# Normalising an octet's attention output in four steps of 128 columns instead of one step of 512

## The reference

```python
xn = _layernorm(x)
x = x + attn0(xn, Wq, Wkv, Wo, bo) + ffn0(xn, ln_w, gate_w, up_w, down_w)
xn = _layernorm(x)
x = x + attn1(xn, Wq, bq, Wk, bk, Wv, bv, Wo, bo) + ffn1(xn, W_gate, W_up, W_down)

# in each attention, for every head
scores  = where(causal, q @ k.T, -inf)
weights = softmax(scores / sqrt(16))
ctx     = weights @ v            # the division by the softmax sum is the step of this case
```

## Time and profile before

| what | us |
|---|---|
| median of 3 runs | 890.82 (888.83 to 896.04) |
| the profiled execution, its own time | 892.07 |
| its span | 889.6 |
| TensorE busy in matmuls | 832.2 (94%) |
| VectorE busy | 607.8 (68%) |
| mean granted TensorE clock | 0.982 of full speed |

### The profile page before, as it was taken

How to read it: one execution, slowest core, us unless ns; L and a number is a source line. 1 busy time by engine, 2 the same in 40 slices (tenths; PEclk the granted TensorE clock), 3 DMA queues, 4 the chain that set the end, 5 groups by cost and what they waited for, 6 DMA issues and landing times.

```text
span 889.6 us, 16314 instructions
## 1 busy us (share of the span) xinstructions
PE 832.2 (94%) x5611; PEld 629.0 (71%) x5612; DVE 607.8 (68%) x1584; ACT 462.0 (52%) x828; POOL 416.0 (47%) x551
## 2 busy tenths in 40 slices
PE   8889999989999898999998998999898998999995
PEld 4866666768867665777787865776578775666785
DVE  7756557797765968666877688575668766665545
ACT  2433555566644555545665465445465564544662
POOL 3233444446444653454443644454355545544543
PEclk9999999999999999999999999999999998999999
DMA  6672363534526263636564274656565384733231
GB/s 204 167 165 73 98 130 129 102 133 78 158 82 165 84 145 101 128 135 128 180 105 173 73 161 139 119 174 103 180 116 162 110 154 148 137 112 102 83 103 48
DMA packets 61841, 113.08 MB, mean 127 GB/s; under 512 B 8760, under 2 KB 11832, under 8 KB 61752
## 3 DMA queue, kind: packets, MB, share of 16 engines
q1 hardware_dynamic: 61760, 112.05, 49.1%
HBM read 87.30 MB, written 24.64 MB: 126 GB/s over the span
## 4 chain that ended last, share of the span: by engine, by line
PE 76%; DVE 15%; issue 3%; ACT 2%; POOL 2%; DMA 1%; POOLq 0%; SPq 0%; ACTq 0%; DVEq 0%
PE g_ring L1226 37%; PE acc L1226 21%; PE s_bank L1339 7%; PE g_ring L1379 6%; PE t_bank L1359 4%; DVE o_t L1215 4%; DVE s_bank L1196 3%; DVE h_lo L1175 2%; DVE x L1183 1%; DVE qk_parts L1134 1%; POOL x L955 1%; DVE context L1216 1%; DVE xn L1111 1%; PE g_ring L1263 1%; POOL w_lo L945 1%
## 5 line engine op out<-in xcount | busy, mean ns | idle before, releaser
L945 POOL TENSOR_TENSOR w_lo<-w_raw,w_hi 128x512 fp32r<-128x512 f32 x204 | 271.3, 1333 | 155.2 <-ACT w_hi L987 150.6
L1196 DVE CUSTOM_DVE_ANT_0 s_bank<-s_bank,causal 128x128 f32<-128x128 f32 (+3 forms) x512 | 236.9, 519 | 36.4 <-PE s_bank L1339 35.9
L967 POOL TENSOR_SCALAR_AFFINE_SELECT p<-p 128x256 f32<-128x256 f32 (+1 forms) x320 | 121.9, 382 | 295.3 <-ACT p L980 288.3
L1226 PE MATMUL g_ring<-xt_hi,w_hi 128*128 128x512 f32 (+1 forms) x504 | 210.8, 418 | 6.2 <-DVE xt_lo L1125 3.2
L1226 PE MATMUL g_ring<-xt_lo,w_hi 128*128 128x512 f32 (+1 forms) x504 | 199.2, 395 | 0.0
L1226 PE MATMUL g_ring<-xt_hi,w_lo 128*128 128x512 f32 (+1 forms) x504 | 198.4, 394 | 0.0
L980 ACT ACTIVATE p<-t_bank 128x512 f32<-128x512 f32 x320 | 173.8, 595 | 36.5 <-PE t_bank L1359 29.7
L987 ACT ACTIVATE w_hi<-w_raw 128x512 fp32r<-128x512 f32 x204 | 127.2, 628 | 112.9 <-PE g_ring L1226 77.7
L1226 PE MATMUL acc<-w_hi,h_hi 128*128 128x256 f32 (+1 forms) x528 | 157.0, 297 | 9.0 <-DVE x L1183 4.9
L1226 PE MATMUL acc<-w_lo,h_hi 128*128 128x256 f32 (+1 forms) x528 | 150.4, 285 | 0.0
L1226 PE MATMUL acc<-w_hi,h_lo 128*128 128x256 f32 (+1 forms) x528 | 150.3, 285 | 0.0
(11 more groups left out here) (86 smaller groups left out, 845.3 us busy)
## 6 DMA issues: line engine op xcount, KB each, us to landing
w_raw<-weights_in SPq DMA_DIRECT2D x204, 256.0 KB, 3.1
qk_scratch<-qk_parts SPq DMA_DIRECT2D x24, 512.0 KB, 2.9
q_op<-qk_scratch SPq DMA_DIRECT2D x96, 128.0 KB, 4.6
o_scratch<-o_t SPq DMA_DIRECT2D x32, 256.0 KB, 3.1
k_op<-qk_scratch SPq DMA_DIRECT2D x48, 128.0 KB, 7.0
context<-o_scratch SPq DMA_DIRECT2D x16, 256.0 KB
o_t<-o_scratch SPq DMA_DIRECT2D x16, 256.0 KB
k_op<-k_scratch SPq DMA_DIRECT2D x48, 64.0 KB, 5.4
```

The source lines that it names most:

```text
L945: pool.tensor_tensor(w_lo[:, c % SPLIT, :], w_raw[:, c % RAW, :], w_hi[:, c % SPLIT, :].bitcast(F32), ALU.subtract).then_inc(split_done, 1)
L967: pool.affine_select(out=view, in_=view, compare_op=ALU.is_ge, fill=0.0, base=0, pattern=[[0, n], [1, P]] if n == 2 else [[1, P]], channel ...
L1196: last = dve.tensor_tensor_reduce(out=bank[:, at:at + n], in0=bank[:, at:at + n], in1=causal[:, 512 - n:], scale=1.0, scalar=LOWEST, op0=A ...
L1226: ins = pe.matmul(dst, w[a], xa[c], start=first and i == 0, stop=last and i == 2, skip_group_check=skip)
```

## The change

The step "norm" of an octet becomes four steps, one for each 128 columns. Each part waits for the same arrival of the read as before, takes its own reciprocal, waits for it, multiplies its own 128 columns, and counts `norm_done` up. The users of a normalised tile wait for the fourth part. In the planner each part is a step of its own, with a cost of 1.35 us where the whole step had 1.3; the four are placed one after the other, each from the planned end of the one before. The expected time of the write to `o_scratch` goes from 5.0 to 4.0 us and that of the read from 10.0 to 8.0. All other steps and their shapes are as they were, but the planner writes all five lists anew.

```diff
-          "norm": 1.3, "hlo": 0.7}
+          "norm": 1.35, "hlo": 0.7}
...
-O_WRITE, O_READ = 5.0, 10.0
+O_WRITE, O_READ = 4.0, 8.0
...
+NORM_PARTS = 4
...
             here = place("sp", free, "oin", octet) + O_READ
-            end["norm", octet] = place("dve", here, "norm", octet)
+            for part in range(NORM_PARTS):
+                end["norm", octet] = here = place("dve", here, "norm", octet, part)
...
-    n_norm = by(numbered(VE, "norm"), 1)
+    n_norm = {s[1]: n for s, n in numbered(VE, "norm").items() if s[2] == NORM_PARTS - 1}
...
                 elif kind == "norm":
-                    octet = s[1]
+                    _, octet, part = s
                     dve.wait_ge(o_here, 32 * (octet + 1))
-                    link(dve.reciprocal(o_t[:, :], o_t[:, :]))
-                    dve.tensor_tensor(context[:, octet % KT, :], context[:, octet % KT, :], o_t[:, :], ALU.mult
+                    at = slice(part * T // NORM_PARTS, (part + 1) * T // NORM_PARTS)
+                    link(dve.reciprocal(o_t[:, at], o_t[:, at]))
+                    dve.tensor_tensor(context[:, octet % KT, at], context[:, octet % KT, at], o_t[:, at], ALU.mult
                                       ).then_inc(norm_done, 1)
```

## The result

The changed kernel takes 909.29 us in the median (907.09 to 913.82, 4 runs), against 891.23 for the kernel before: a ratio of 1.0202 with a 95% interval of 1.0144 to 1.0261. It is 18 us slower. The forecast was 886 with a range of 866 to 903, so the sign was wrong and the time lies above the range.

The account below looks back on a forecast made before the run. TensorE was taken to bound the kernel, waiting behind the norms on VectorE. Covers −10, arrivals +8.3, end +1.9 and clock −9 + 4 made −4.8 us from 892.07, so 887.3, or 886 us against the median; range 866 to 903.

Parts of the forecast that it names:

- The bound: Whole kernel: TensorE bounds it, and VectorE work counts by TensorE's waits, 24.1 us idle behind the 16 norms, plus clock drops.
- the ceiling: Behind the norms: what they cost now, about 33 us of TensorE idle and clock drops, as the most any gain could be.
- the term of the longer block: On VectorE at each norm: four parts take 4.9 us, 0.8 us longer than 4.1, bounds 0.4 and 1.2 us.
- the six octets with 6.5: Octets 0, 1, 4, 8, 9, 13, with 6.5 us of TensorE work around the norm: 1.9 us idle each, 11.4 in all.
- the three middle ones: Octets 6, 10 and 11, with middling TensorE work around the norm: claimed to idle 1 us together.
- The clock: TensorE's clock behind the norms: drops costing 9 us now shrink to 4 us, with the mean clock near 0.988.
- Rival (c): At the norms: the new order brings nothing, only the longer block costs, 9 us plus 1.9 at the end; 902 us, chance 0.09.
- The covers: TensorE steps that run while a norm blocks VectorE: longer ones in the new lists were to win 10 us.
- such a stall away from the norms: In TensorE's new list outside the norms: a sign that the prediction is wrong; no size was given.
- The arrival: Read before the norm's first part: VectorE waits 17.6 us for late data, costing TensorE 8.3 us, bounds 0 and 17.6.
- Rival (b): At the norm's first part: late reads block VectorE, some 35 us of waits; 906 us, 900 to 916, chance 0.13.
- The end: Last group: octet 15's norm ahead of the two xadd loses 1.9 us, and 1.2 to 2.1 more if the clock drops.

## Why the prediction was wrong

**The bound was right.** TensorE waits behind the norms, and with the norm halved the old lists lose 26 us of the 33 that were given as the ceiling.

**The step that failed is the term of the longer block: "the block is 0.8 us longer than 4.1", charged at "the six octets with 6.5" and hardly anywhere else.** The prediction charged it with 5.8 us of idle (0.8 at each of the six short octets, 1 at the three middle ones). In the runs the same lists with one block and with four parts differ by 15.0 us of idle and 21 us of time, and on the old lists the division costs 17 us. Two things were wrong in it.

Its size: the block is 1.2 us longer, at the upper bound given. Undisturbed, four parts do take 4.9 us as worked out; what was left out is GpSimd. A product of 128 columns was put at 332 ns, takes 0.29 us alone and 440 ns in the mean. The trace of before held the hint in a row that the prediction quoted, 860 ns in the mean where the timeline has 690, and the prediction named it as a way to be wrong, but not as a term. Over the 17 traces there are 576 products: the 185 that run beside no GpSimd instruction are within 3 ns of the least of their shape, and the 232 that are over 10% above it all run beside one, 220 of them beside a split of weights. The excess has a size, too: 239 products start while one split runs, and 237 of these are longer than their least, within 20 ns, by what is left of the split less 0.14 us, and by nothing where less than that is left. At octet 12 the split has 1.04 us left when the first product starts, so 0.29 + 1.04 − 0.14 = 1.19, and 1.18 is measured. No run took GpSimd's work away, but these rows leave little room for another cause. The Trainium skill's "GPSIMD Engine Reference" says, in its table of specifications, that GpSimd's SBUF interfaces are shared with VectorE, with contention for VectorE's instructions of two SBUF inputs, which the product is; it gives no price. The trace agrees.

Its place: the longer block was charged almost only where no wait for the read was expected, and the waits mostly apart from it, though both use up the same cover. By the prediction's own numbers (a need of 8.4 us, a cover of 11.3) the waits of 5.8 and 4.2 us leave 2.9 us of idle at octet 12 and 1.3 at octet 7, where it wrote "hide all but about 1 us"; measured are 2.6 and 3.2. At octets 6, 7, 10, 11 and 12 the longer block cost 8.8 us of idle where the prediction had 1; at the six short ones 5.4 where it had 4.8.

Two more terms were off. The clock was to give back 5 us, and matmuls took 2.1 us more; 3.5 us of this is the block's doing too, as with one block they took 1.4 us less. And TensorE idles 3.4 us more away from the norms, which the prediction put at nothing. With the 9.3 us in the stretches (9.5 measured, 0.2 forecast) these 7.1 and 3.4 make up the whole difference of 19.8 us between the forecast of −4.8 us and the +15.0 of the span.

Rival (c), short tiles only cost, at 902 and a chance of 0.09, came nearest in its mechanism: with one block the new lists take the time of the old ones, and the longer block is what is left. It has 11 of the 18 us, since it too took 0.8 us for the block, in eleven octets. The page that the prediction drew on, the Trainium skill's "VectorE: DVE Perf Modes" with its section on the TRN2 errata, asks for 512 elements or more and pointed the right way. The about 75 ns per instruction of the Trainium skill's "Vector Engine (DVE) Microarchitecture Reference" (rate slope and fixed cost) is half of what the reciprocals alone show, where each waits for the one before: (4 × 944 − 3344)/3 = 144 ns for each further one.

**The covers** came out nearly as sized. New lists with one block against the old ones are the test: TensorE's idle in the stretches is 18.6 us and not 24.1, so 5.5 less, and the prediction's own arithmetic with a block 0.8 us shorter gives the same (−15.7 from covers, +8.3 from arrivals, +1.9 at the end); part of so close a match is luck. But the time is 888.2 against 890 or so: outside the stretches TensorE idles 3.0 us more (36.3 for 33.3), with six more waits for the maxima's rows, 5.9 us, and its matmuls take only 1.4 us less. The prediction named such a stall away from the norms as a sign of being wrong.

**The arrival** was sized well in VectorE's time: 17.6 us forecast, 19.0 measured, at octets 6, 7, 10, 11, 12 and 13 and a little at 3. Its price of 8.3 us stands beside the 7.7 us that moving five norms gave back (888.20 to 880.49), but that move also changed what stands behind the block, so the price is not shown. Rival (b), nearest in its time (906), was wrong as a mechanism: with the same 18.9 us of waiting one block takes 888.

**The end** went as written in the trace: one wait of 5.2 us for the two xadd and a clock of 0.75 in the stretch. That it cost time is not shown: with the last norm moved back the time is the same.

**The clock** went the other way. Instead of rising to 0.988, the mean fell from 0.982 to 0.978. Stalls of 2.4 to 5.2 us remained in eight octets where three were foreseen, and half clock was granted behind six of them (1, 7, 10, 11, 12 and 15), for 31 us in all where it was 24 us behind six norms before. Behind octet 6, with an idle of 3.3 us, it stayed at 1.00, so the idle in a stretch alone does not tell where it falls.

## What to carry to other kernels

An engine with idle time of its own can still carry the bound through the length of one undivided block; count what is added to it at about one us per us (21.1 us for 19.1 here), and set its length together with any wait ahead of it against the cover. Cost an instruction from its mean in the trace and not from its best case where the two differ. Splitting a step whose parts then stood back to back only made it longer; with other steps between the parts it did not gain here either, at 901 and 907 us. Look for new waits over the whole program, not only where the edit is. Where a planner's constants are changed with an edit, run the edit on the old lists and the new lists without the edit: here the two together told the parts, 17 to 21 us, from the lists, under 2.

## What the hardware showed that was not expected

A product of 128 columns with two inputs from SBUF takes 0.29 us beside no work of GpSimd and up to 1.29 us beside it; the same product over 512 columns takes 0.69 to 1.83. So a product that finds a split running waits until that is nearly over, whatever its own length, and the four short ones of an octet can each meet one. Four of the short ones lost 0.6 us in the mean per octet (64 at 440 ns, 292 alone), one long one 0.17 (16 at 860 ns, 692 alone). The reciprocal, with one input, kept its time within 2% (0.94 to 0.96 us for 128 columns). A write of 256 KB issued by ScalarE landed in 2.0 to 11.1 us with a median of 3.8, no sooner than from SyncE's queue (2.0 to 10.7, median 2.5 in the changed kernel).
